# Input tiles of the next batch, normalised inside the attention: fetched by SP, with two buffers, wider gaps between the steps, and half a staging buffer

## What is computed

```python
def _layernorm(x, axis=-1, eps=1e-05):
    m = jnp.mean(x, axis=axis, keepdims=True)
    v = jnp.var(x, axis=axis, keepdims=True)
    return (x - m) / jnp.sqrt(v + eps)
...
        qkv = jnp.einsum('bse,ef->bsf', x, W_qkv)
        qkv = qkv.reshape(batch, seq_len, 3, NUM_HEADS, HEAD_DIM)
        q, k, v = (qkv[:, :, 0], qkv[:, :, 1], qkv[:, :, 2])
        q = rotary_embedding(q, seq_len, HEAD_DIM)
        k = rotary_embedding(k, seq_len, HEAD_DIM)
        scores = jnp.einsum('bqhd,bkhd->bhqk', q, k) * scale
        scores = jnp.where(mask, scores, NEG_INF)
        weights = jax.nn.softmax(scores, axis=-1)
        out = jnp.einsum('bhqk,bkhd->bqhd', weights, v)
...
    x = x + _L0_attn_ref(_layernorm(x, axis=-1), L0_attn_W_qkv, L0_attn_W_out)
    x = x + _L0_xattn_ref(_layernorm(x, axis=-1), ctx_1024, ctx_1024, ...)
    x = x + _L0_ffn_ref(_layernorm(x, axis=-1), ...)
```

## Time and profile before

| | |
|---|---|
| median of 3 runs | 3186.05 us (3177.39 to 3186.2) |
| profiled execution | 3181.87 us, span 3180.1 us |
| attention | about 100 to 1763 us of the span |
| busy over the span | PE 87%, PE weight loads 73%, DVE 63%, ACT 52%, POOL 48% |
| granted TensorE clock | 0.944 of full |
| DMA | 100 GB/s in the mean |

### The profile page before, as it was taken

How to read it: one execution, slowest core, us unless ns; L and a number is a source line. 1 busy time by engine, 2 the same in 40 slices (tenths; PEclk the granted TensorE clock), 3 DMA queues, 4 the chain that set the end, 5 groups by cost and what they waited for, 6 DMA issues and landing times. The chain is left out here.

```text
span 3180.1 us, 49756 instructions
## 1 busy us (share of the span) xinstructions
PE 2781.7 (87%) x15887; PEld 2317.8 (73%) x15887; DVE 1993.6 (63%) x3907; ACT 1669.0 (52%) x3190; POOL 1520.2 (48%) x1630
## 2 busy tenths in 40 slices
PE   5889889998889989899998478988874999999998
PEld 3778768877777777688887366767663888888886
DVE  5566656666656666666666367777764566556565
ACT  2455555655555555565666232232222666667665
POOL 1566554656555656455555134334432444444444
PEclk8999989999999999899999699999986999999999
DMA  3634343434343433424334434454434444444432
GB/s 116 134 85 112 82 112 88 109 85 114 83 107 96 103 97 97 111 73 103 88 74 97 114 95 126 114 116 123 117 90 147 96 93 99 96 96 93 99 60 46
DMA packets 219177, 316.80 MB, mean 100 GB/s; under 512 B 60048, under 2 KB 138928, under 8 KB 215664
## 3 DMA queue, kind: packets, MB, share of 16 engines
q1 hardware_dynamic: 174416, 213.91, 27.5%
q0 software_dynamic: 44576, 100.60, 13.0%
HBM read 241.28 MB, written 75.17 MB: 100 GB/s over the span
## 5 line engine op out<-in xcount | busy, mean ns | idle before, releaser
L1003 ACT ACTIVATE a_pt<-a_PT 128x512 fp32r<-128x512 f32 (+3 forms) x768 | 351.6, 490 | 633.0 <-PE a_PT L874 632.4
L1078 DVE TENSOR_REDUCE a_nmax<-a_S 128x1 f32<-128x1024 f32 (+7 forms) x512 | 385.7, 753 | 260.7 <-PE a_S L863 260.7
L1087 DVE TENSOR_TENSOR a_pt<-a_PT,a_pt 128x512 fp32r<-128x512 f32 (+3 forms) x768 | 401.4, 550 | 234.1 <-ACT a_pt L1003 233.0
L891 PE MATMUL a_O<-a_pt,a_v 128*128 128x256 f32 (+1 forms) x2560 | 361.9, 289 | 51.8 <-DVE a_ot L1102 35.7
L874 PE MATMUL a_PT<-a_ident,a_pb 128*128 128x128 f32 x2304 | 350.7, 280 | 59.6 <-DVE a_pt L1087 56.4
L992 ACT ACTIVATE a_pb<-a_S,a_nmax 128x1024 f32<-128x1024 f32 (+7 forms) x512 | 380.2, 743 | 16.1 <-DVE a_nmax L1078 16.0
L891 PEld LDWEIGHTS a_O<-a_pt,a_v 128*128 128x128 f32 x2560 | 330.7, 196 | 72.8 <-DVE a_ot L1102 46.5
L1969 DVE TENSOR_TENSOR e_w<-e_raw,e_w 128x1024 fp32r<-128x1024 f32 x238 | 280.8, 1220 | 121.6 <-ACT e_w L1919 121.4
L874 PEld LDWEIGHTS a_PT<-a_ident,a_pb 128*128 128x128 f32 x2304 | 276.1, 144 | 106.4 <-DVE a_pt L1087 36.3
L811 PE MATMUL a_Z<-early_xT,early_wq 128*128 128x512 f32 x512 | 244.5, 477 | 46.6 <-DVE a_tmp L1052 17.7
L730 POOL TENSOR_TENSOR a_rot<-a_tmp,a_rot 128x512 fp32r<-128x512 f32 x128 | 162.5, 1290 | 256.6 <-ACT a_rot L975 256.2
(11 more groups left out here) (287 smaller groups left out, 7073.1 us busy)
## 6 DMA issues: line engine op xcount, KB each, us to landing
a_qs<-a_rot SPq DMA_DIRECT2D x256, 128.0 KB, 2.3
a_kh<-a_rot SPq DMA_DIRECT2D x256, 128.0 KB, 2.3
a_kl<-a_rot SPq DMA_DIRECT2D x256, 128.0 KB, 2.3
e_rows<-scr_hs SPq DMA_DIRECT2D x40, 516.0 KB
scr_attT<-a_ot SPq DMA_DIRECT2D x256, 64.0 KB, 2.1
m_att<-scr_attT SPq DMA_DIRECT2D x32, 512.0 KB, 4.3
m_rb<-scr_rinv SPq DMA_DIRECT2D x64, 256.0 KB, 8.9
a_raw<-in_wqk POOLq DMA_DIRECT2D x31, 512.0 KB, 4.1
```

The costliest lines, as they stand in the source:

```text
L891: mm = pe.matmul(O[:, c0:2 * P], v2[:, n % 2, kt, h, :, :].rearrange("p a d -> p (a d)"), pt[j % 2][:, part, kt, c0:2 * P], start=kt == 0 ...
L1003: act.activation(pt[u % 2][:, 0, 4 * s:4 * s + m, (qt % 2) * P:(qt % 2 + 1) * P], PT[(k + s) % 2][:, 0:m * P].rearrange("p (k q) -> p k q" ...
L1078: dve.tensor_reduce(nmax[:, u % GU:u % GU + 1], S[u % 2][:, 0:cols], AXX, ALU.max, negate=True).then_inc(s_nb, 1)
L1087: dve.tensor_tensor(pt[u % 2][:, 1, 4 * s:4 * s + m, q], PT[(k + s) % 2][:, 0:m * P].rearrange("p (k q) -> p k q", k=m), pt[u % 2][:, 0, 4 ...
```

## The change

The input tiles' steps are spaced out and moved between queues. `TILES` becomes (3, 15, 27, 35, 47, 59, 67, 79). SP fetches a tile at T, in place of POOL, into one of two buffers `xt`; VectorE takes the statistics at T + 4, POOL normalises at T + 5, TensorE transposes the halves at T + 9 and T + 13 and does so at the end of the unit, behind both halves of `fill`; VectorE copies a half in the unit after (T + 10, T + 14), and SP stores each half by itself one unit later (T + 11, T + 15). `xs` shrinks from four blocks of 128 columns to two, and each copy waits for the store before it. The number of stores doubles, each has half the bytes. Instructions of the arithmetic are the same.

```diff
--- before.py
+++ after.py
@@ -403,8 +403,8 @@
         scl = rm.sb("scl", [P, 1])
         tmp = rm.sb("tmp", [P, 2, 2, 512])
         part = rm.sb("part", [P, 2, 512])
-        xt = rm.sb("xt", [P, D])
-        xs = rm.sb("xs", [P, D])
+        xt = rm.sb("xt", [P, 2, D])
+        xs = rm.sb("xs", [P, 2, P])
         bst = rm.sb("bst", [P, 6])
         mv = rm.sb("mv", [P, 2])
         nw = rm.sb("nw", [P, 5])
@@ -461,7 +461,7 @@
-        s_x = rm.sem("x")
+        s_x = [rm.sem(f"x{i}") for i in range(2)]
@@ -544,7 +544,7 @@
 
             return sum(max(0, (u - 1 - d) // QT + 1) for d in TURN)
 
-        TILES = (3, 15, 27, 39, 51, 63, 75, 87)
+        TILES = (3, 15, 27, 35, 47, 59, 67, 79)
 
         def tile_in(u, lag):
 
@@ -641,11 +641,16 @@
                     sp.dma_start(dram["rinv"][g * GH:(g + 1) * GH, b:b + 1, :, :].rearrange("h o q p -> h (o q) p"),
                                  rT[g * GH * QT:(g + 1) * GH * QT, :]).then_inc(s_rst, 16)
 
-            def store_tile(m):
+            def fetch_tile(m):
+                if m >= 2:
+                    sp.wait_ge(s_xt, 2 * m - 2)
+                sp.dma_start(xt[:, m % 2, :], io["x"][T + m * P:T + (m + 1) * P, :]).then_inc(s_x[m % 2], 16)
+
+            def store_tile(m, a):
                 b, t = m // QT + 1, m % QT
-                sp.wait_ge(s_xs, 2 * m + 2)
-                sp.dma_start(dram["xnT"][b:b + 1, :, t * P:(t + 1) * P].rearrange("o (e p) t -> p (o e) t", p=P),
-                             xs[:, :].rearrange("p (e t) -> p e t", e=ET)).then_inc(s_xst, 16)
+                sp.wait_ge(s_xs, 2 * m + a + 1)
+                sp.dma_start(dram["xnT"][b:b + 1, a * 2 * P:(a + 1) * 2 * P, t * P:(t + 1) * P]
+                             .rearrange("o (e p) t -> p (o e) t", p=P), xs[:, :, :]).then_inc(s_xst, 16)
 
             stack(0)
             stack(1)
@@ -668,12 +673,15 @@
                     stack(u // QT + 1)
                 if sums_turn(u - 1) is not None:
                     store_sums(sums_turn(u - 1))
-                if tile_in(u, 10) is not None:
-                    store_tile(tile_in(u, 10))
+                if tile_in(u, 0) is not None:
+                    fetch_tile(tile_in(u, 0))
+                for a in range(2):
+                    if tile_in(u, 11 + 4 * a) is not None:
+                        store_tile(tile_in(u, 11 + 4 * a), a)
             sp.wait_ge(s_rst, 16 * G * B)
             for i in range(4):
                 sp.wait_ge(s_ost[i], 16 * NPAIR // 4)
-            sp.wait_ge(s_xst, 16 * QT * (B - 1))
+            sp.wait_ge(s_xst, 32 * QT * (B - 1))
 
         @block.gpsimd
         def _(gp):
@@ -693,7 +701,7 @@
                     else:
                         gp.wait_ge(s_wlow, wcount[q])
                 if p[0] == "x":
-                    gp.wait_ge(s_xst, 16 * QT * p[1])
+                    gp.wait_ge(s_xst, 32 * QT * p[1])
                     src = dram["xnT"][p[1], p[2] * P:(p[2] + 1) * P, :]
                 elif p[0] == "wq":
                     src = io["wqk"][pair_of(p[1])]
@@ -730,11 +738,6 @@
                     gp.tensor_tensor(rot[:, 2 + r, cols], tmp[:, c, r, :], rot[:, r, cols].bitcast(F32),
                                      ALU.subtract).then_inc(s_rot, 1)
 
-            def fetch_tile(m):
-                if m:
-                    gp.wait_ge(s_xt, 2 * m)
-                gp.dma_start(xt[:, :], io["x"][T + m * P:T + (m + 1) * P, :]).then_inc(s_x, 16)
-
             rs = Chain(gp, s_rstd)
             rs.step(gp.memset(nw[:, 4:5], -0.5))
 
@@ -747,7 +750,7 @@
                 rs.step(gp.tensor_tensor(nw[:, 2:3], nw[:, 2:3], nw[:, 0:1], ALU.mult))
                 rs.step(gp.tensor_scalar(nw[:, 2:3], nw[:, 2:3], -0.5, 1.5, ALU.mult, ALU.add))
                 rs.step(gp.tensor_tensor(nw[:, 3:4], nw[:, 1:2], nw[:, 2:3], ALU.mult))
-                gp.tensor_scalar(xt[:, :], xt[:, :], mv[:, 0:1], nw[:, 3:4], ALU.subtract,
+                gp.tensor_scalar(xt[:, m % 2, :], xt[:, m % 2, :], mv[:, 0:1], nw[:, 3:4], ALU.subtract,
                                  ALU.mult).then_inc(s_xn, 1)
 
             for c in range(2):
@@ -789,10 +792,8 @@
                     rope_low(i, c)
                 for p in splits(u):
                     low(p)
-                if tile_in(u, 0) is not None:
-                    fetch_tile(tile_in(u, 0))
-                if tile_in(u, 3) is not None:
-                    norm_tile(tile_in(u, 3))
+                if tile_in(u, 5) is not None:
+                    norm_tile(tile_in(u, 5))
                 if u == 9:
                     context_start()
                 if u % (2 * QT) in (11, 14):
@@ -902,7 +903,7 @@
                     pe.wait_ge(s_ofree, values_done(u))
                 for k in range(2):
                     mm = pe.transpose(O[:, (2 + k) * P:(3 + k) * P],
-                                      xt[:, (2 * a + k) * P:(2 * a + k + 1) * P], ident[:, :])
+                                      xt[:, m % 2, (2 * a + k) * P:(2 * a + k + 1) * P], ident[:, :])
                 mm.then_inc(s_xt, 1)
 
             def fill(u, late):
@@ -933,18 +934,18 @@
                     z_ready(("s", b, 0))
                     pe.wait_ge(s_exp, GU * G * (b + 1))
                     pe.transpose(zbank(("s", b, 0))[:, 0:P], rsum[:, b % 2, :], ident[:, :]).then_inc(s_zfull, 1)
-                for a in range(2):
-                    if tile_in(u, 5 + 4 * a) is not None:
-                        turn_tile(u, tile_in(u, 5 + 4 * a), a)
                 fill(u, 0)
                 if 2 <= u < U + 2:
                     turn(u - 2)
                 fill(u, 1)
+                for a in range(2):
+                    if tile_in(u, 9 + 4 * a) is not None:
+                        turn_tile(u, tile_in(u, 9 + 4 * a), a)
                 if values_turn(u) is not None:
                     for a in range(2):
                         for lag in range(1, 4):
-                            if tile_in(u, 5 + 4 * a + lag) is not None:
-                                pe.wait_ge(s_xs, 2 * tile_in(u, 5 + 4 * a + lag) + a + 1)
+                            if tile_in(u, 9 + 4 * a + lag) is not None:
+                                pe.wait_ge(s_xs, 2 * tile_in(u, 9 + 4 * a + lag) + a + 1)
                     values(values_turn(u))
 
         @block.scalar
@@ -1052,8 +1053,8 @@
                 dve.tensor_tensor(out[1], zbank(z)[:, :], second[:, cols], ALU.mult).then_inc(s_zfree, 1)
 
             def tile_stats(m):
-                dve.wait_ge(s_x, 16 * (m + 1))
-                dve.bn_stats(bst[:, :], xt[:, :]).then_inc(s_bn, 1)
+                dve.wait_ge(s_x[m % 2], 16 * (m // 2 + 1))
+                dve.bn_stats(bst[:, :], xt[:, m % 2, :]).then_inc(s_bn, 1)
                 dve.wait_ge(s_bn, m + 1)
                 if m:
                     dve.wait_ge(s_xn, m)
@@ -1061,9 +1062,9 @@
 
             def tile_out(m, a):
                 dve.wait_ge(s_xt, 2 * m + a + 1)
-                if m:
-                    dve.wait_ge(s_xst, 16 * m)
-                dve.tensor_copy(xs[:, a * 2 * P:(a + 1) * 2 * P], O[:, 2 * P:4 * P]).then_inc(s_xs, 1)
+                if m + a:
+                    dve.wait_ge(s_xst, 16 * (2 * m + a))
+                dve.tensor_copy(xs[:, :, :].rearrange("p e t -> p (e t)"), O[:, 2 * P:4 * P]).then_inc(s_xs, 1)
 
             def v_low(n, j):
                 dve.wait_ge(s_vhi, 4 * n + j + 1)
@@ -1110,11 +1111,11 @@
                     rowmax(u)
                 if values_turn(u - 1) is not None:
                     out_add(values_turn(u - 1))
-                if tile_in(u, 2) is not None:
-                    tile_stats(tile_in(u, 2))
+                if tile_in(u, 4) is not None:
+                    tile_stats(tile_in(u, 4))
                 for a in range(2):
-                    if tile_in(u, 5 + 4 * a) is not None:
-                        tile_out(tile_in(u, 5 + 4 * a), a)
+                    if tile_in(u, 10 + 4 * a) is not None:
+                        tile_out(tile_in(u, 10 + 4 * a), a)
                 for i, j in ends(q_steps(u - 1), 4):
                     rope_mult(i, j)
                 if sums_turn(u) is not None:
```

## The result

The changed kernel takes 3225.74 us (median of 4 runs, 3218.26 to 3229.05), the kernel before 3185.13 us beside it (3177.39 to 3186.2): ratio 1.013, with a 95% interval of 1.0105 to 1.0154. It is slower by 41 us. The forecast was slower, 3267 us; the range 3215 to 3300 holds the result.

What follows compares the result with a forecast made beforehand. The prediction took stalls of order, not a full engine, as the bound; terms of -68, +61, +67, +12.7, +8 and +4.5 gave +85 us on the profiled 3181.87 us, so 3267 us, range 3215 to 3300.

Steps and rivals of the forecast that it cites:

- Part 1: Tile-work stalls at units 42, 68 and 90 go (62 us), with the first tile's (6 us): gain 68 us.
- Part 2: Tiles 15, 47, 79: the copy into `xs` waits for a store issued behind `stack`; 6.8 us, nine times: 61 us.
- Part 3: Tiles 35 and 67: normalisation makes `stack` late, so the awaited store lands later; 11.2 us, six times: 67 us.
- 4, first fetch: Tile 0's fetch stands behind SP's 32 loads; VectorE waits 12 us for it: cost 12.7 us (10 to 15).
- Part 5: `values` waiting for the copy after the transposes, 8 us, and VectorE's statistics meeting `rope_mult`, 4.5 us.
- The statistics at phase 7: In units numbered 7 modulo 16, VectorE's statistics meet `rope_mult`: nine tiles by 0 to 1 us, 4.5 us.
- (a): Half-tile stores land in time, so VectorE's copies in units of phase 13 never wait: 3139 us, faster; chance 0.12.
- (b): POOL's normalisation at phase 8 doesn't delay `rope_low`, so all fifteen stalls cost 6.8 us: 3241 us; chance 0.17.
- (c): TensorE's clock holds through part of the fifteen store-wait gaps, 2.2 us less each: 3234 us; chance 0.06.
- (d): Which queue issues the fetches and stores makes no difference; gains and losses cancel: 3182 us; chance 0.03.

Runs made afterwards that it cites:

- e2: The changed kernel with SP's half-tile stores issued ahead of `stack` in the same unit: 3128.8 us, 0.983 of the kernel before.
- e4: The changed kernel with tile 0's fetch ahead of SP's 32 loads: 3212.12 us, 1.009 of the kernel before.
- e6: The changed kernel with both the stores ahead of `stack` and the first fetch ahead of SP's 32 loads: 3120.73 us, 0.9804 of the kernel before.
- e7: e6 with the transposes back at the head of the unit and the copy in the same unit: 3108.03 us, 0.977 of the kernel before.
- e8: The kernel before with the new `TILES`, and POOL fetching the first tile ahead of its loop: 3114.36 us, 0.9789 of the kernel before.
- e3: The changed kernel with POOL's normalisation at T + 6 instead of T + 5: 3199.49 us, 1.0047 of the kernel before.
- e9: e7 with the fetches moved back to POOL, two buffers kept, the first ahead of POOL's loop: 3104.22 us, 0.9769 of the kernel before.
- e1: The changed kernel with `xs` of two halves, a semaphore each, and `ot` cut from four buffers to three: 3130.71 us, 0.9831 of the kernel before.

## Why the prediction was right, and where it was off

The direction and every place were right: fifteen waits of the copy for the store, in the units of phase 13; one wait for the first fetch; none at w = 42, 68 and 90. The sum of the parts was +85 against a measured +47 in the span, so more than a third of the loss that was forecast did not come; the range held the result because its low end had been drawn from smaller terms. By the parts, each measured as the difference of after and before in its own units:

| part | forecast, us | measured, us | where |
|---|---|---|---|
| 1, what goes | -68 | -68 | w = 42, 68, 90 and the units behind -61.7, w = 6 and 7 of the first batch -6.2 |
| 2, nine stalls | +61 | +47 | w = 29, 61, 93 and the units behind; also 40.0 over e2, and 9 x 0.8 that e2 keeps |
| 3, six stalls | +67 | +57 | w = 45, 77; also 52.6 over e2, and 6 x 0.8 |
| 4, first fetch | +12.7 | +11 | w = 8 and 9 of the first batch; after to e4 11.1 there, e2 to e6 13.4 |
| 5, small ones | +12.5 | about -1 | w = 13, 37 and 69 +5.5, all other units -6.1 |

**Part 1** was right stall by stall and not only in the sum: 6.6, 7.4 and 6.5 us in the mean at w = 42, 68 and 90, where I took 6.9, and 6.2 for the first tile, where I took 6.

**Parts 2 and 3** had the right mechanism; each of their terms was somewhat too big. (i) The end of `stack`: I took it 1.95 us after the mask, the middle of the earlier trace rows, and it was 1.44; in Part 3 I took 8.4 us for the twelve and a start 1.5 us before the mask, and it took 7.55 to 7.77 from 1.95 before it. The short `stack` was not one end of a range but the usual case (twelve of fifteen). (ii) The landing: 2.6 us by the earlier trace rows, where the store had 256 KB; the halved one takes 2.1. (iii) The clock: 2.2 us per stall from stalls of 4.2 to 5.2 us in the earlier trace rows. Part 2's nine cost 5.3 us each, of which 3.8 are the delay (4.35 against 0.52), so the clock took 1.4 in the mean, and in the unit shown nothing; in Part 3 9.6 less 7.9, 1.7. Together 14 and 10 us. The ends of the ranges that the text kept (3.7 to 5.5 of delay, half the clock's part) hold these values.

**Part 5** failed: nothing was left of its 12.5 us. The delay of `values` behind the copy is real: 0.8 us at phase 13, for which I had read 1.1, and it is worth 12 us in all (e6 against e7); but nearly all of it lies in the fifteen units of Parts 2 and 3. I added 8 us for other units, where +0.8 at w = 13 and +0.54 at w = 37 and 69 came to 5.5, and small gains in many units took them back (-0.2 at phases 1 and 9, -0.4 to -0.6 in the mean at w = 8, 20 and 56). The statistics at phase 7 (4.5 us) left no cost that shows. And I had no term for a gain from the new phases, which the 7.3 us between e8 and e7 show.

**Rivals.** (a) fell: no store landed in time. (b) fell by e3. (c) was true in one of the fifteen gaps, the one at 753.34, where the clock held; behind most of the others it cost less than 2.2 us. Its 3234 is nearest to the result, which is luck: it stands for a reason that makes up only some 10 of the 38 us. (d), the queue is indifferent, fell in its sum, though e9 bears it out for the fetches: e2 changes nothing but the order of issues in one engine's program, and is 97 us faster.

**The skill.** Moving 24 fetches from SP to POOL (e9) changed nothing, and in that the trace agrees with the Trainium skill, "DMA: Bandwidth & Descriptors", "Issuing engines are not separate DMA queues". One issue of 0.6 us is small beside the 2.1 us to landing; twelve of them ahead of the store (7.55 us) are not, and taking the store from behind them was worth 97 us (e2). The landing of 2.1 us for 128 KB lies nearer to the estimate of 2.3 us by "Anatomy of one DMA" of the same page of the Trainium skill than to the 2.6 us that I took from the row of the 256 KB store. That section gives its figures for transfers issued by GpSimd, which the prediction didn't say, and this store is issued by SP, so the estimate was not made for it.

## What to carry over

A buffer that is halved turns its store into something that is waited for: look at once at what stands ahead of that store in the issuing engine's program, for here reordering two statements was worth as much as a second buffer (e1 and e2). Before steps are moved between queues or spaced out, see whether the stalls lie in a table of start times; one line of numbers gave 1.9% here, and the queue nothing. A step put at the end of a unit to be out of the way delays whoever waits for its result at the start of the next.

## What the runs showed of the chip

TensorE's clock after a gap was less regular than the earlier trace rows made it look. Behind a gap of 3.2 us it stayed at 2.4 GHz in one unit (753.34) and in another (the same stall at tile 15, w = 29 of the second batch, TensorE idle to 644.41) it fell to 1.2 GHz for 3.4 us, and only 1.5 us after the matmuls had set in again. At w = 61 of the third batch a gap of 3.2 us was followed by 6.8 us at 1.2 GHz. In the gap of 7.83 us it fell 2.2 us after TensorE had stopped and stayed low for 10.2 us, 5.7 of which lay within the gap; so a gap twice as long did not cost twice the clock. By unit lengths over e2, less the delay of `values`, the clock took 0 to 2.3 us per stall, 1.4 in the mean of the nine and 1.7 in that of the six; this is better than the single value of 2.2.

The twelve transfers of `stack` took 7.55 us in most units of phase 10 and 8.5 to 9.1 in some, with the same instructions, about 0.6 us an issue. What lengthens them in some units stays open; no run tried it.
